# The place of the output projection in a gated-linear-attention stage: behind the first pair of output-gate projections instead of in front of it

## The reference, cut to what matters

```python
q = (x @ Wq.T).reshape(b, s, H, DH)          # H = 16 heads of DH = 64, HID = 1024
k = (x @ Wk.T).reshape(b, s, H, DH)
v = (x @ Wv.T).reshape(b, s, H, DH)
log_decay = -softplus(x @ Wd.T + bd)
gate = sigmoid((x @ Wg.T).reshape(b, s, H, DH))
out = gla_scan(q, k * gate, v, log_decay)    # s_t = exp(g_t) s_{t-1} + k_t v_t ; o_t = q_t s_t
out = out.reshape(b, s, HID)
out = out * rsqrt(mean(out * out, -1) + eps) * norm_w
out = out * sigmoid(x @ Wog.T)               # the output gate
return out @ Wo.T                            # the output projection
```

## Time and profile before

| what | value |
|---|---|
| median of 3 runs | 2045.75 us (2045.68 to 2047.19) |
| the profiled execution's own time | 2044.7 us |
| its span in the profile | 2042.8 us |
| granted TensorE clock, mean over the span | 0.983 of full speed |
| TensorE busy | 1971.9 us, 97% |
| VectorE busy | 1624.4 us, 80% |
| ScalarE busy | 1269.4 us, 62% |
| GpSimd busy | 619.6 us, 30% |

### The profile page before, as it was taken

How to read it: one execution, slowest core, us unless ns; L and a number is a source line. 1 busy time by engine, 2 the same in 40 slices (tenths; PEclk the granted TensorE clock), 3 DMA queues, 4 the chain that set the end, 5 groups by cost and what they waited for, 6 DMA issues and landing times. The chain is left out here.

```text
span 2042.8 us, 42619 instructions
## 1 busy us (share of the span) xinstructions
PE 1971.9 (97%) x17138; PEld 1398.5 (68%) x17138; DVE 1624.4 (80%) x2545; ACT 1269.4 (62%) x2554; POOL 619.6 (30%) x477
## 2 busy tenths in 40 slices
PE   7999999999999999998999999999999999889997
PEld 6743333333333346987888888888888888778896
DVE  7789999999999987997667676667666666667774
ACT  3248888888888877776554545454545454535453
POOL 2200000101010014543434353425343434145454
PEclk9979999999999999998999999999999999989999
DMA  6832223222322313315322222222222222322231
GB/s 230 256 64 63 59 70 73 72 55 74 68 73 54 92 47 99 116 53 153 98 75 84 74 84 74 84 75 84 75 83 75 83 75 84 97 89 99 89 115 73
DMA packets 103350, 180.63 MB, mean 88 GB/s; under 512 B 24217, under 2 KB 65713, under 8 KB 98033
## 3 DMA queue, kind: packets, MB, share of 16 engines
q1 hardware_dynamic: 103152, 177.91, 28.7%
HBM read 138.41 MB, written 38.67 MB: 87 GB/s over the span
## 5 line engine op out<-in xcount | busy, mean ns | idle before, releaser
L743 DVE TENSOR_REDUCE att_sb_mx<-att_ps_psM 128x1 f32<-128x1024 f32 x512 | 624.2, 1221 | 26.8 <-PE att_ps_psM L982 24.0
L1196 ACT ACTIVATE att_sb_pt<-att_ps_psSO 128x512 f32<-128x512 f32 x1024 | 557.1, 597 | 94.1 <-PE att_ps_psSO L1000 39.2
L982 PE MATMUL att_ps_psM<-stack_sb_k,stack_sb_q 48*128 48x512 f32 x1024 | 381.8, 454 | 4.9 <-DVE att_sb_mx L743 3.2
L1000 PE MATMUL att_ps_psSO<-stack_sb_q,stack_sb_k 50*128 50x512 f32 x1024 | 373.1, 444 | 0.0
L1012 PE MATMUL att_ps_psSO<-att_sb_pt,stack_sb_v 128*32 128x256 f32 x4096 | 326.4, 391 | 8.6 <-ACT att_sb_osb L1189 8.6
L1000 PEld LDWEIGHTS att_ps_psSO<-stack_sb_q,stack_sb_k 50*128 50x128 f32 x1024 | 153.1, 184 | 201.7 <-ACT att_sb_pt L1196 155.5
L1012 PEld LDWEIGHTS att_ps_psSO<-att_sb_pt,stack_sb_v 128*32 128x32 f32 x4096 | 82.0, 108 | 192.1 <-issue 102.5
L2977 POOL TENSOR_TENSOR glan_sb_dm<-glan_sb_dm,glaa_sb_masked 128x1024 f32<-128x1024 f32 x64 | 172.4, 2713 | 31.2 <-DMA glan_sb_dm<-decay_rows 31.1
L2551 ACT ACTIVATE glag_sb_sg<-att_ps_psM 128x512 f32<-128x512 f32 x64 | 38.3, 599 | 222.7 <-PE att_ps_psM L2294 222.6
L982 PEld LDWEIGHTS att_ps_psM<-stack_sb_k,stack_sb_q 48*128 48x128 f32 x1024 | 157.0, 189 | 19.1 <-DVE att_sb_mx L743 16.6
L2568 ACT ACTIVATE glan_sb_dm<-glan_sb_dm,glaa_sb_neg_g 128x128 f32<-128x128 f32 x512 | 156.5, 393 | 0.2
(11 more groups left out here) (354 smaller groups left out, 5141.8 us busy)
## 6 DMA issues: line engine op xcount, KB each, us to landing
glan_sb_dm<-decay_rows SPq DMA_DIRECT2D x32, 1024.0 KB, 5.6
qk_parts<-stack_sb_part SPq DMA_DIRECT2D x32, 512.0 KB, 3.3
glai_sb_eg<-decay_exp SPq DMA_DIRECT2D x64, 256.0 KB, 6.3
stack_sb_q<-qk_parts SPq DMA_DIRECT2D x192, 64.0 KB, 3.0
stack_sb_k<-qk_parts SPq DMA_DIRECT2D x96, 128.0 KB, 4.3
att_sb_rb<-sums SPq DMA_DIRECT2D x32, 256.0 KB
attended<-att_sb_on SPq DMA_DIRECT2D x32, 256.0 KB, 5.0
moem_sb_gb<-gate_rows SPq DMA_DIRECT2D x4, 2048.0 KB, 7.4
```

The lines of the kernel that those rows point to most:

```text
L743: nc.vector.tensor_reduce(mx[:, qh, 8 * r + c:8 * r + c + 1], psM[:, t % 2, :], AX.X, ALU.max).then_inc(maxima_taken, 1)
L982: mm = pe.matmul(psM[:, t % 2, c * ST:(c + 1) * ST], q[rs, g, qh, j, n * P:(n + 1) * P], k[rs, g, j, c * ST:(c + 1) * ST], start=True, sto ...
L1000: pe.matmul(psS[:, ring_slot(pos), :], k[rs, g, j, s * P:(s + 1) * P], q[rs, g, qh, j, :], start=True, stop=True).then_inc(ring_done, 1)
L1196: nc.scalar.activation(pt[:, s % (LAG + 2), ORDER[i], :], psS[:, (pos + 1) % 3, :], ACT.Exp, scale=AD ** -0.5).then_inc(ring_taken, 1)
```

## The change

The call of `out_project(c)` in TensorE's `half_supertile` moves from in front of the four output-gate pairs to behind the first of them. No instruction is added or removed, and the orders of the other four engines stay as they are.

```diff
                 pair(jp, wq, q_done)
-            if c is not None:
-                out_project(c)
             for jp in range(PAIRS):
                 if i == 0 and hf == 0 and jp == 0:
                     pe.wait_ge(w_lo_ready, 10)
                 if jp < 2:
                     pe.wait_ge(q_ready, base + jp + 3)
                 else:
                     pe.wait_ge(og_ready, base + jp - 1)
                 pair(jp, wog, og_done)
+                if jp == 0 and c is not None:
+                    out_project(c)
                 if turning and jp % 2:
```

## The result

| | time | against before |
|---|---|---|
| before | 2045.09 us, median of 20 runs (2042.04 to 2048.07) | |
| changed | 2048.79 us, median of 20 runs (2045.77 to 2054.16) | ratio 1.0022, 95% interval 1.0015 to 1.0028 |
| forecast | 2050.4 us on a base of 2045.75, that is + 4.65 us | 1.0023 |

The kernel became slower by 0.22%, 4.5 us by the ratio, 3.7 us by the medians. The whole interval, 3.1 to 5.7 us, is a loss.

A forecast was written before the change was run, and what follows sets the result against it. TensorE was taken to bound the GLA stage. Stalls of 8.17 us go and 12.82 us come at 15 places, + 4.65 us on the median 2045.75, giving 2050.4 us; range 2048.0 to 2053.4.

The forecast's parts named there:

- The bound: In the GLA stage TensorE sets the pace, busy 198.71 of 200 us, so its waits come out one to one.
- rival 2: No change that can be told: about 0.1 us less per place, loss 3.15 us, 2048.9 us; chance 0.24.
- What goes: At the output projection's first matmul, TensorE's stall for VectorE's `y_lo` disappears at all 15 places, 8.17 us.
- What is late next: First gate pair waits for ScalarE's copy of query pair 2: 8 x 0.79 and 7 x 0.93, 12.82 us.
- The release: TensorE starts 0.05 us after the copy of query pair 2 ends; at most 0.09 us more per place.
- The new step: From first gate pair into output projection: taken as 0, bounds 0 to 1.65 us over 15 places.
- rival 3: Costlier: exposed restart at gate pair to output projection (1.65) plus slower release after the copy (1.35), 2053.4 us; chance 0.15.
- The waits behind: Behind the moved block, third gate pair (2.6 us in hand) and VectorE's mean square (4.59 us cover) cost 0.
- The exponentials: Eight on ScalarE before the copy of query pair 2 take 2.43 us by the row, 3.3 by the skill page.
- Rival 1: Copy of query pair 2 in time, so no new stall replaces that for `y_lo`: -8.17 us, 2037.6; chance 0.06.

The follow-up runs named there:

- all sixteen exponentials first: ScalarE does all sixteen exponentials, not eight, before copying query pair 2: on the changed kernel 2103.39 us, ratio 1.0277; on the kernel before, ratio 1.0013.
- the later exponentials: Each group of eight exponentials on ScalarE stands one query-pair copy later: on the changed kernel 2035.27 us, ratio 0.9949; on the kernel before 2044.69 us, ratio 0.9999.
- the two edits: Moved output projection alone, ratio 1.0022; each group of eight exponentials one copy later on the kernel before, 0.9999; both together, 0.9949.

## Why the prediction was right

- **The bound.** That the stage goes at TensorE's pace held: over 14 places the working has 4.57 us, and the stage grew by 4.40. The time of the runs alone would not show it, since its interval (3.1 to 5.7 us) holds rival 2's 3.15 us as well. That the forecast time of 2050.4 lies 1.6 us over the measured 2048.79 is for 0.7 us the base, 2045.75 from three runs, where 20 runs gave 2045.09.
- **What goes.** The wait for `y_lo` went at all 15 places, as worked out.
- **What is late next.** The stalls from start to start are 0.78 or 0.79 us at the 8 places behind n = 1 and 0.93 at the 7 behind n = 3, together 12.82 us; forecast were 0.79, 0.93 and 12.82. The view's counts are 0.62 to 0.63 and 0.76 to 0.77 us (0.6 and 0.8).
- **The release.** 0.63 us from the start of the copy to TensorE's start was measured at place after place (0.62 to 0.64). The 0.09 us more that the first `half_supertile` allowed did not come at the 15 places. They belong to that one place, and not to the late weights alone, to which the view puts its wait down: with all sixteen exponentials first, in either order of TensorE, the weights are there over 1 us before the copy ends, and the gate pair still starts 0.72 or 0.73 us after the start of the copy. It is the only place whose first gate pair waits for two semaphores, one after the other; that this is the reason is likely, and not shown.
- **The new step.** The output projection follows the gate pair after 0.11 or 0.12 us at every place: the 1.65 us of rival 3 are 0.
- **The waits behind.** None at the third gate pair (3.1 us in hand, where the forecast has 2.6), none at the next scores. The mean square's wait of 0.70 us was not named in the forecast as a wait of its own, but its cover was.
- **The exponentials.** In front of the copy the group took 2.44 us again, and eight more lengthened each stall by 2.34 us. The 3.3 us that the forecast worked out as an estimate from the Trainium skill ("ScalarE: Activation LUTs", Rules for kernel authors) are eight times the budget for one. The budget fits one exponential by itself (0.39 us recorded, 0.41 by the budget); what the estimate left out is that they overlap: in the row the next one starts 0.29 us after the one before.
- **The rivals.** Rival 1 needed copies 0.8 us earlier; the later exponentials put them 1.4 us earlier or more, and the gain of the other side came, on top of the loss undone. The change had only half of what it takes. Its price of 8.17 us was too small, since it left out the 15 restarts that go with the stalls, some 0.10 us each.
- **What was too narrow.** The spread. The forecast took it from three runs that lay 1.5 us apart, and 4.1 us as what can be told from no change; 20 runs lie 6 to 8 us apart, and only their number makes 4 us visible.

## What to carry to other kernels

Before work is moved away from a wait, list the waits of what comes up in its place: a block that looks like the victim of one wait may be the cover of another. Write down when each engine releases each of them; here the two ends lay 0.13 us apart in the example behind n = 1 and up to 0.8 us behind n = 3, where most of the loss comes from, and their order decided the sign. Here two engines share a ring of two buffers, and the order on one side was only worth something together with the order on the other: the two edits cost 0.22% and 0, and gained 0.5% together.

## What the runs showed of the hardware

- With all exponentials first on the changed kernel, TensorE waited 3.11 to 3.27 us (from start to start) in the middle of dense work at 15 places. At nine of them the granted clock fell to 0.50 for 3.4 us, beginning 0.5 to 1.5 us after the wait had ended (matmuls 0.21 us apart); at two it was 0.50 from within the wait on, for 6.8 us; at four it stayed at 1.00. Waits of 2.8 us in the first `half_supertile` were followed by the half clock too, in both kernels that have them. Stalls of 0.93 us were not, at any place. The loss from the clock, 19 us, was a good half of that from the longer waits, 35 us.
- At full clock a matmul restarted after a wait has its successor 0.22 to 0.23 us behind it instead of 0.12; a block whose waits are met long before it joins on at 0.12.
- From the recorded end of a ScalarE copy to the start of the matmul that waits for it, 0.05 to 0.06 us.
- Exponentials of 128 columns in a row on ScalarE start 0.29 us apart, while each is recorded 0.39 us long.
